# Gate rows stored and broadcast by GpSimd instead of SyncE in a two-layer expert tower

## What is computed

```python
e = stack([tbl_f[ids[:, f]] for f in range(5)], axis=1)      # (1024, 5, 1024)

def ple_layer(x, W, b, Gw, Gb, Gsw=None, Gsb=None):          # T=4 tasks, 10 experts
    xe = x[:, min(arange(10) // 2, 4), :]                    # experts 8, 9 are shared
    eo = relu(einsum('bed,edh->beh', xe, W) + b)
    gates = softmax(einsum('btd,tdk->btk', x[:, :4, :], Gw) + Gb)
    task_out = einsum('btk,btkh->bth', gates, eo[:, SEL, :]) # own two and shared two
    if Gsw is None:
        return task_out
    gs = softmax(x[:, 4, :] @ Gsw + Gsb)
    shared_out = einsum('be,beh->bh', gs, eo)
    return concatenate([task_out, shared_out[:, None, :]], axis=1)

z = ple_layer(ple_layer(e, W0, b0, G0w, G0b, Gs0w, Gs0b), W1, b1, G1w, G1b)
h = relu(concatenate([z.reshape(1024, -1), dense_ctx], axis=1) @ W_top1 + b_top1)
y = relu(h @ W_top2 + b_top2) @ W_top3
```

## Time and profile before

| | |
|---|---|
| median of 3 runs | 2047.74 us (2043.83 to 2049.45) |
| the profiled execution | 2042.9 us, of which the span is 2041.1 |
| TensorE busy | 2013.5 us, 99% of the span |
| VectorE busy | 1372.1 us, 67% |
| ScalarE busy | 716.4 us, 35% |
| GpSimd busy | 169.2 us, 8% |
| DMA | 230.44 MB, mean 113 GB/s |
| granted TensorE clock | 0.999 |

### The profile page before, as it was taken

One profiled execution on the slowest core, in us unless ns is written; L12 is line 12 of the kernel. 1 busy time (PEld: TensorE's weight loads), 2 busy tenths in 40 slices (PEclk: granted clock), 3 DMA queues, 4 the chain that ended last, 5 costly groups with the idle time before them and its releaser, 6 DMA issues.

```text
span 2041.1 us, 26192 instructions
## 1 busy us (share of the span) xinstructions
PE 2013.5 (99%) x8832; PEld 1640.8 (80%) x8832; DVE 1372.1 (67%) x1427; ACT 716.4 (35%) x964; POOL 169.2 (8%) x152
## 2 busy tenths in 40 slices
PE   7999999999999999999999999999999999999999
PEld 6878787888878888888887787888888888888887
DVE  4579888887256765658555888887953667566564
ACT  3333233323333333333434333323233332423343
POOL 4631000000030002111033000000000000000000
PEclk9999999999999999999999999999999999999999
DMA  6544333333343334334344333243333323332321
GB/s 194 171 147 124 114 93 116 90 126 101 97 138 110 107 94 136 118 125 123 93 145 133 115 93 122 84 134 110 101 102 93 107 90 119 98 112 94 113 94 42
DMA packets 70003, 230.44 MB, mean 113 GB/s; under 512 B 12398, under 2 KB 12654, under 8 KB 69948
## 3 DMA queue, kind: packets, MB, share of 16 engines
q1 hardware_dynamic: 61688, 208.75, 32.6%
q0 software_dynamic: 7488, 20.98, 3.2%
q10 hardware_dynamic: 772, 0.09, 0.0%
HBM read 229.56 MB, written 0.23 MB: 113 GB/s over the span
## 4 chain that ended last, share of the span: by engine, by line
PE 88%; DVE 5%; issue 3%; DMA 3%; ACT 1%; SPq 0%; ACTq 0%; POOL 0%; DVEq 0%
PE main L336 26%; PE main L338 26%; PE main L337 26%; PE top L336 3%; PE top L337 3%; PE top L338 3%; DVE w_lo L769 1%; DMA gate_b<-gates_dram 1%; PE gps L373 1%; PE gps L371 1%; DVE prod L844 1%; DMA gates_dram<-logit_t 1%; DVE eo_b L844 1%; ACT w_hi L478 0%; DMA eo_sh<-in_tbl,idx 0%
## 5 line engine op out<-in xcount | busy, mean ns | idle before, releaser
L336 PE MATMUL main<-act_hi,w_hi 128*128 128x512 f32 x2568 | 1002.1, 390 | 15.5 <-DVE w_lo L769 9.4
L337 PE MATMUL main<-act_lo,w_hi 128*128 128x512 f32 x2568 | 1000.1, 389 | 0.0
L338 PE MATMUL main<-act_hi,w_lo 128*128 128x512 f32 x2568 | 1000.1, 389 | 0.0
L769 DVE TENSOR_TENSOR w_lo<-raw,w_hi 128x1024 fp32r<-128x1024 f32 (+1 forms) x356 | 433.7, 1218 | 555.1 <-ACT w_hi L478 554.9
L478 ACT ACTIVATE w_hi<-raw 128x1024 fp32r<-128x1024 f32 (+1 forms) x356 | 376.3, 1057 | 1117.4 <-PE main L338 1016.4
L336 PEld LDWEIGHTS main<-act_hi,w_hi 128*128 128x128 f32 x2568 | 482.2, 188 | 132.3 <-issue 11.1
L338 PEld LDWEIGHTS main<-act_hi,w_lo 128*128 128x128 f32 x2568 | 482.4, 188 | 101.3
L337 PEld LDWEIGHTS main<-act_lo,w_hi 128*128 128x128 f32 x2568 | 482.3, 188 | 99.6
L850 DVE TENSOR_TENSOR slots<-slots,prod 128x1024 f32<-128x1024 f32 (+1 forms) x200 | 244.8, 1224 | 5.9
L327 POOL DMA_INDIRECT slots<-in_tbl,idx x144 | 165.1, 1147 | 929.9 <-DVE act_lo L781 616.9
L844 DVE TENSOR_TENSOR prod<-eo_sh,gate_b 128x1024 f32<-128x1024 f32 x136 | 165.7, 1218 | 4.7 <-DMA gate_b<-gates_dram 2.8
(11 more groups left out here) (67 smaller groups left out, 584.2 us busy)
## 6 DMA issues: line engine op xcount, KB each, us to landing
raw<-in_w SPq DMA_DIRECT2D x320, 512.0 KB, 3.6
gate_b<-gates_dram SPq DMA_DIRECT2D x34, 512.0 KB, 4.7
raw<-in_w_top SPq DMA_DIRECT2D x32, 512.0 KB, 3.5
gate_b<-gates_dram SPq DMA_DIRECT2D x16, 256.0 KB, 4.3
slots<-in_tbl,idx POOLq DMA_INDIRECT x144, 3.5
raw<-in_w_top SPq DMA_DIRECT2D x4, 256.0 KB, 2.7
eo_b<-in_dense SPq DMA_DIRECT2D x2, 192.0 KB, 2.7
gates_dram<-logit_t SPq DMA_DIRECT2D x18, 12.0 KB
```

The lines of the kernel that those rows point to most:

```text
L336: nc.tensor.matmul(dst, lhs_hi, rhs_hi, start=start, stop=False)
L337: nc.tensor.matmul(dst, lhs_hi, rhs_lo, start=False, stop=False)
L338: return nc.tensor.matmul(dst, lhs_lo, rhs_hi, start=False, stop=stop)
L769: nc.vector.tensor_tensor(w_lo[0:parts, slot, 0:cols], raw[0:parts, rawslot, 0:cols], w_hi[0:parts, slot, 0:cols], ALU.subtract).then_inc( ...
```

## The change

`gates_round` is taken out of SyncE's list and put into GpSimd's, with the same four parts. SyncE's list keeps the weight units and the loads of gate weights. On GpSimd the rounds stand at places given by the table `rounds`: after the gathers of group (half, task, group) the rounds (half, number) listed there. Round 0 of the first half stands after the four groups of task 0, round 1 after the first group of task 3, rounds 2 to 4 after its last group. Round 5 stands after the second group of the second half's task T, and so on; round 0 of the second half stands after the second group of task 2, and its rounds 1 to 8 after the last gather.

```diff
-            def gates_round(Q, parts, Pb):
-
-                sp.wait_ge(rows_rdy, Q + 1)
-                sp.dma_start(gates_dram[bass.ds(Q, 1), :].rearrange("a (j n) -> (a j) n", j=GROWS),
-                             logit_t[0:GROWS, :]).then_inc(gates_out, 16)
-                sp.wait_ge(gates_out, Q * 16 + 16)
-                if not isinstance(Pb, int) or Pb:
-                    sp.wait_ge(pair_done, Pb)
-                for lo, hi in parts:
-                    sp.dma_start(gate_b[:, lo:hi, :].rearrange("p j n -> p (j n)"),
-                                 gates_dram[bass.ds(Q, 1), lo * N:hi * N].broadcast_to([P, (hi - lo) * N]))\
-                        .then_inc(gates_in[lo // 2], 16)
...
-            def gated_stream(src, first, U, off, Q, parts, Pb, g=None, start=0):
+            def gated_stream(src, first, U, off, Q, g, start=0):
 
                 stream(src, first, STEP // 2, U, off, start)
-                if g is not None:
-                    gate_load(g, Q + 1)
-                gates_round(Q, parts, Pb)
+                gate_load(g, Q + 1)
                 stream(src, first + STEP // 2, STEP // 2, U + STEP // 2, off)
...
-                gates_round(gated + 2 * T, FOR_L1, p1 + 8 * (T - 1))
...
+            FOR_SHARED, FOR_L0, FOR_L1 = ((4, 6),), ((0, 2), (2, 4), (4, 6)), ((1, 2), (2, 4), (4, 5))
+
+            def gates_round(h, n):
+
+                Q, Pb = h * GATED + n, h * PAIRS + 8 * n
+                pool.wait_ge(rows_rdy, Q + 1)
+                pool.dma_start(gates_dram[Q:Q + 1, :].rearrange("a (j n) -> (a j) n", j=GROWS),
+                               logit_t[0:GROWS, :]).then_inc(gates_out, 16)
+                pool.wait_ge(gates_out, Q * 16 + 16)
+                if Pb:
+                    pool.wait_ge(pair_done, Pb)
+                for lo, hi in FOR_SHARED if n == 0 else FOR_L0 if n <= T else FOR_L1:
+                    pool.dma_start(gate_b[:, lo:hi, :].rearrange("p j n -> p (j n)"),
+                                   gates_dram[Q:Q + 1, lo * N:hi * N].broadcast_to([P, (hi - lo) * N]))\
+                        .then_inc(gates_in[lo // 2], 16)
...
+            rounds = {(0, 0, 3): ((0, 0),), (0, 3, 0): ((0, 1),), (0, 3, 3): ((0, 2), (0, 3), (0, T)),
+                      (1, T, 1): ((0, T + 1),), (1, T, 3): ((0, T + 2),), (1, 0, 0): ((0, T + 3),),
+                      (1, 1, 0): ((0, 2 * T),), (1, 2, 1): ((1, 0),),
+                      (1, 3, 3): tuple((1, n) for n in range(1, GATED))}
...
+                        for which in rounds.get((h, t, bt), ()):
+                            gates_round(*which)
```

More of the change, by code:

```diff
@@ L246, in top2 @@
                     unit(w_top2, d, (U + d) % RAW, U + d, cols=2 * TOP2)
-            FOR_SHARED, FOR_L0, FOR_L1 = ((4, 6),), ((0, 2), (2, 4), (4, 6)), ((1, 2), (2, 4), (4, 5))
-            def gated_stream(src, first, U, off, Q, parts, Pb, g=None, start=0):
+            def gated_stream(src, first, U, off, Q, g, start=0):
                 stream(src, first, STEP // 2, U, off, start)
-                if g is not None:
-                    gate_load(g, Q + 1)
-                gates_round(Q, parts, Pb)
+                gate_load(g, Q + 1)
                 stream(src, first + STEP // 2, STEP // 2, U + STEP // 2, off)
@@ L267, in _ @@
                         unit(w0, c, c, c)
-                gated_stream(w0, 0, first, first % RAW, gated, FOR_SHARED, p0, g=0, start=1 if h == 0 else 0)
+                gated_stream(w0, 0, first, first % RAW, gated, g=0, start=1 if h == 0 else 0)
                 if h:
@@ L271, in _ @@
                 with sp.Fori(0, T) as t:
-                    gated_stream(w0, STEP + t * STEP, base + U_T0 + t * STEP, base % RAW, gated + 1 + t, FOR_L0, p0 + 8 + t * 8,
-                                 g=t + 1)
+                    gated_stream(w0, STEP + t * STEP, base + U_T0 + t * STEP, base % RAW, gated + 1 + t, g=t + 1)
                 stream(w1, 0, STEP // 2, base + U_SH1, base % RAW)
@@ L278, in _ @@
                 off = (base + U_T1) % RAW
-                p1 = p0 + 8 * (T + 1)
-                gated_stream(w1, STEP, base + U_T1, off, gated + T + 1, FOR_L1, p1, g=T + 1)
+                gated_stream(w1, STEP, base + U_T1, off, gated + T + 1, g=T + 1)
                 with sp.Fori(0, T - 2) as t:
                     gated_stream(w1, 2 * STEP + t * STEP, base + U_T1N + t * (STEP + MT1), off, gated + T + 2 + t,
-                                 FOR_L1, p1 + 8 + t * 8, g=T + 2 + t)
+                                 g=T + 2 + t)
                     stream(w_top, t * MT1, MT1, base + U_T1N + STEP + t * (STEP + MT1), off)
```

## The result

The changed kernel takes 2051.0 us by the median of 20 runs (2049.4 to 2053.5); the kernel before, run 20 times, takes 2045.9 (2042.6 to 2049.5). The ratio is 1.0025, 95% interval 1.0018 to 1.0032: slower by 5.1 us. The profiled execution took 2049.9 us, its span is 2047.8, 6.7 us more than that of before. The code moved a little in the file: L336 of before is L338, L478 is L480, L769 is L771, L819 is L821, L844 is L846, L850 is L852, L870 is L872; the round's store is L285 and its broadcast L291. Rows of the experiments have the lines of their own kernels.

A forecast was written before the change was run, and what follows sets the result against it. TensorE's waits for split weights behind layer 0's eight gate rounds were taken as the bound: 9.8 us gained, 12.2 lost in three late rounds, 2.4 slower, giving 2050.1 us on the median; range 2044 to 2062.

The forecast's parts named there:

- What bounds the kernel, and the eight waits: Layer 0: TensorE's eight waits for split weights behind the gate rounds all go, 9.8 us gained.
- The longer path, D = 1.2: Every round: store plus broadcast by GpSimd take 1.2 us more than SyncE's pair, 0.6 for each.
- First shared step, 1.6 us: First half: store 2.6 us later behind gathers, 3.8 with the longer path; 2.2 covered, 1.6 us reach TensorE.
- Second shared step, 7.1 us: Second half: store 5.9 us later behind gathers, 7.1 with the longer path, no cover, all lost.
- First layer-1 step, 3.5 us: First half: store 2.5 us later, second gate later still; 0.6 covered, 3.1 to 3.9 lost, 3.5 taken.
- The other seven rounds of layer 1: GpSimd idle there, the store earlier by more than the longer path; they stay free for TensorE.
- VectorE holds up GpSimd's DMAs: Rival, five layer-0 rounds: w_lo delays GpSimd's store and perhaps broadcast; 7.4 us slower, 2055.1 us, chance 0.20.
- Much longer path: Rival, GpSimd's store plus broadcast: 2.0 us or more longer than SyncE's; 7.3 us slower, 2055.0 us, chance 0.15.
- no longer path: Rival, GpSimd's store plus broadcast: no longer than SyncE's; loss 8.6, gain 9.8, 1.2 us faster, 2046.5 us, chance 0.12.

The follow-up runs named there:

- run 20: No label of a follow-up: the kernel before, unchanged, was run 20 times; median 2045.9 us (2042.6 to 2049.5).
- all three: Changed kernel with three late rounds (round 0 of each half, first layer-1 round of the first half) moved ahead of gathers: 2030.7 us, ratio to before 0.9928.
- the first alone: Changed kernel with only round 0 of the first half moved, from behind task 0's fourth gather group to behind its second: 2040.5 us, ratio to before 0.9974.
- The spaced kernel: Against the kernel with three late rounds moved: GpSimd waits for a round's first broadcast to land before issuing the other two; 2030.3 us in one run.

## Why the prediction was right or wrong

The time was right: 2050.1 foretold, 2051.0 measured, in the direction forecast and within the 6.1 us named as no difference to be told. With 20 runs the measurement told 5.1 us from none all the same. The hit is in part luck. The difference to before was foretold as 2.4 us and measured as 5.1, and three errors nearly cancelled: the loss was 20.0 us and not 12.2 (7.8 more), the gain by the medians 20.0 - 5.1 = 14.9 and not 9.8 (5.1 more), and the median of three runs, on which the sum was put, stood 1.8 us above that of twenty (7.8 - 5.1 - 1.8 = 0.9). One term, the first shared step, was wrong by more than the whole difference.

- **What bounds the kernel, and the eight waits.** Right. All eight went. They were worth 11.9 us in the units and 15 or more by the medians, against 9.8. Two things were missing. Each wait costs about 0.25 us beyond its idle time ((11.9 - 9.8) / 8): a matmul's modelled duration of 0.39 us is 0.16 longer than the regular distance of 0.23 to the next, and the first after a stop has 0.47. And one profile showed before in one of its better executions.
- **The longer path, D = 1.2.** Mis-sized, in both legs and with opposite signs. The store by GpSimd took 2.0 to 2.4 us to the next issue (one of 18 took 3.2), not the 2.6 to 3.5 of SyncE plus 0.6. Its own row says 1.8 us to landing. SyncE's store put two units earlier took 1.4 to 1.7, which fits that before it stood behind weight units in its queue; no run isolates that. The broadcast leg is longer by 1.0 us in the step of the earlier trace rows (5.3 against 4.3), by 1.0 to 2.0 in the five steps like it, by 1.9 to 2.6 in layer 1 (603.43 - 597.43 = 6.0 in its first step, against 3.4), and shorter in the second shared step, where one goes alone (1060.11 - 1056.42 = 3.7 against 4.8). Over both legs, from store to first multiplication, D was 0.15 us in the step of the earlier trace rows (7.33 against 7.18), 0.2 to 1.3 in the five, 0.7 in their mean, 1.6 in the first layer-1 step, and -1.0 and -1.6 in the shared steps.
- **First shared step, 1.6 us.** This step of the sum failed: 1.6 us foretold, 10.5 measured. The last row of the fourth gather group was to be read; the row at 39.43 of the earlier trace rows ends the third. In the trace of before the fourth group starts at 45.54 and its last instruction at 49.48, so the round had to be 12 us late and not 2.6. Counting the groups against the table `begin` (0, 1, 2, 4 units) would have shown it: a group that waits for four units can't start when only two are done. The kernel with the round after the third group ran what the prediction had priced, and there the loss is none.
- **Second shared step, 7.1 us.** The size was right (6.6) by luck, by two errors that met. The store came 5.6 us later than SyncE's and the path was 1.6 shorter, which leaves about 4 us, of which 3.8 are the wait; the rest of the 6.6, 2.8, is the clock, which the prediction didn't have.
- **First layer-1 step, 3.5 us.** Right to 0.6 (2.95). The first gate held it up and not the second: the three broadcasts left 0.54 us apart, not 1.25. The gathers' spacing was no measure for a plain DMA.
- **The other seven rounds of layer 1.** Right, no wait.
- **VectorE holds up GpSimd's DMAs.** Fell. The stores of the five layer-0 rounds start 0.35 us into a `w_lo`, and take 0.52 us, as all 18 do (0.522 to 0.572); a gather of the changed kernel at 173.29, 0.36 us into an addition of VectorE, took 1.68. At the very start of a `w_lo` (34.67) a gather (34.69) took 1.98. It fits what the Trainium skill (SBUF — State Buffer, section SBUF: two separate sides) says: two SBUF inputs of VectorE shut out a GpSimd instruction only where that reads SBUF. A gather reads its indices, a plain DMA doesn't.
- **Much longer path; no longer path.** Neither was the case: over the 15 steps in which VectorE waits for the gate D ran from -1.6 to 2.2, by the kind of step. In the shared steps the path was no longer; but the time of that rival, 2046.5, was not the one measured, because its losses held the same misread row.
- **The start.** The first units took 1.2 us less in the profile of after than in that of before, with a higher clock from 15 to 25 us. Seen over all profiles this goes with the execution and not with the change: before, its second profile and two of the moved kernels (all three, and the first alone) have the longer first unit, the others the shorter.

## What to carry to other kernels

An engine that only gathers looks free, but its list has its own waits: an urgent step put behind a paced one inherits that one's release, here the end of TensorE's fourth unit. Before an engine is changed, ask whether the same step a little earlier on its old engine does it; two weight units were worth as much as the change with its places put right. Read off which group a row belongs to by counting from the start against the code's wait values, and price a stop of TensorE with the clock that may follow it.

## What the runs showed of the hardware that was not expected

**The clock after a stop.** A wait of TensorE of 8.8 us was followed by a stretch at 0.59 of the clock and cost 10.5 us; one of 3.8 us by 0.50 and 0.72 and cost 6.6. The same place in the kernel with only the first round moved had a wait of 4.0 us at 0.76 and 0.82 and cost 5.7. Shorter waits went either way: those of 2.7 us in the second profile of before and 2.6 below had a lower clock behind them, and even one of 1.84 us had, while one of 1.9 us in before (237.48) had not. In the changed kernel the one at 608 us left the clock at 1.00. In the kernel with only the first round moved it was the same place and nearly the same wait:

```profile
598.85 0.76 PE L338 MATMUL main<-act_hi,w_hi 128*128 128x512 f32 x1 [2.60 <-DVE w_lo L771]
```

```profile
600.00:604.00 4.00, 4.00 (x15) 3.17 (x14) 4.00 (x4) 0.00 (x0) 0.00 (x0) 0.74 0.52 145
```

There the unit was 4.4 us longer, not 2.95. So the length of the wait alone doesn't decide it here. What does was not tried.

**A plain DMA of GpSimd** occupies it for 0.54 us where a gather takes 0.95, and a 12 KB store from it lands in 1.8 us. With three broadcasts at once the first gate is in use 5.0 to 6.3 us after the first issue, in the 13 task steps where VectorE waits for it, against 3.7 to 4.7 for a single one in the shared steps. Not every step has it: in the three layer-0 steps in which VectorE turns gathered rows the gate is there within 4.6 us with three at once. The spaced kernel speaks for crowding as part of it; why SyncE's three don't suffer as much is open.
